# Attention and expert layer: all shared tiles first, routed results added to the output in place

## The reference

```python
x = x + xattn(layernorm(x), ctx, ...)
h = layernorm(x)
shared = gelu(h @ shared_up) @ shared_down                # 256 -> 1024 -> 256
probs = softmax(h @ router_w)                             # 8 experts
top_k_prob, top_k_idx = top_k(probs, 2)
routed = sum over the two chosen e of gate[e] * (gelu(h @ routed_up[e]) @ routed_down[e])
out = x + (shared + routed + h)
```

## Time and profile before

| | |
|---|---|
| time, median of 3 executions | 2223.13 us (2220.79 to 2226.14) |
| time of the profiled execution | 2221.47 us |
| its span in the profile | 2219.8 us |
| mean granted clock of TensorE | 0.995 |
| TensorE busy (matmuls) | 2157.2 us, 97% |
| VectorE busy | 1799.5 us, 81% |
| ScalarE busy | 1351.4 us, 61% |
| GpSimd busy | 293.9 us, 13% |

### The profile page before, as it was taken

One profiled execution on the slowest core, in us unless ns is written; L12 is line 12 of the kernel. 1 busy time (PEld: TensorE's weight loads), 2 busy tenths in 40 slices (PEclk: granted clock), 3 DMA queues, 4 the chain that ended last, 5 costly groups with the idle time before them and its releaser, 6 DMA issues. The chain is left out here.

```text
span 2219.8 us, 48796 instructions
## 1 busy us (share of the span) xinstructions
PE 2157.2 (97%) x18002; PEld 1579.6 (71%) x18002; DVE 1799.5 (81%) x2416; ACT 1351.4 (61%) x1914; POOL 293.9 (13%) x300
## 2 busy tenths in 40 slices
PE   6999999999999999999999999999997999999998
PEld 5666666666666666666666666655886999999997
DVE  7999989899899988989989998897534555557777
ACT  6675676567567566656756755564443555567773
POOL 2110000011011000000100100001572121121120
PEclk9999999999999999999999999999998999999999
DMA  7235335334423523533442363132563434336656
GB/s 265 89 116 163 89 111 176 91 95 145 133 86 121 175 80 98 177 102 97 129 145 88 102 197 91 49 110 87 200 227 117 133 129 136 133 126 221 225 186 267
DMA packets 149314, 305.62 MB, mean 138 GB/s; under 512 B 34784, under 2 KB 71776, under 8 KB 146080
## 3 DMA queue, kind: packets, MB, share of 16 engines
q1 hardware_dynamic: 138688, 272.46, 39.2%
q0 software_dynamic: 10176, 30.45, 3.8%
q10 hardware_dynamic: 288, 0.26, 0.0%
HBM read 189.31 MB, written 79.20 MB: 121 GB/s over the span
## 5 line engine op out<-in xcount | busy, mean ns | idle before, releaser
L1030 ACT ACTIVATE probs<-scores 128x1024 f32<-128x1024 f32 x512 | 503.3, 1025 | 331.6 <-PE scores L745 326.3
L871 PE MATMUL sum_ps<-probs,v_nat 128*64 128x512 f32 x2056 | 479.2, 599 | 9.3 <-DVE probs L1229 9.3
L1335 DVE TENSOR_TENSOR sums<-sums,probs 128x1024 f32<-128x1024 f32 x384 | 470.2, 1224 | 12.5
L745 PE MATMUL scores<-q_split,k_split 64*128 64x512 f32 x3072 | 415.5, 395 | 1.8 <-ACT probs L1030 1.8
L1229 DVE TENSOR_SCALAR probs<-probs 128x2048 f32<-128x2048 f32 x256 | 313.1, 1223 | 100.5 <-ACT probs L1030 99.1
L1917 PE MATMUL sum_ps<-down,hid_split 128*128 128x256 f32 x2640 | 353.8, 284 | 7.5 <-DVE acc L2060 3.9
L1917 PEld LDWEIGHTS sum_ps<-down,hid_split 128*128 128x128 f32 x2640 | 341.1, 191 | 26.2 <-issue 7.3
L1894 PE MATMUL scores<-xT,up 128*128 128x512 f32 (+1 forms) x1680 | 348.1, 349 | 0.0
L745 PEld LDWEIGHTS scores<-q_split,k_split 64*128 64x128 f32 x3072 | 282.6, 185 | 57.0 <-ACT probs L1030 5.9
L2051 DVE TENSOR_TENSOR hid_split<-hid,hid_split 128x512 fp32r<-128x512 f32 x205 | 142.1, 693 | 217.9 <-ACT hid_split L1981 217.4
L871 PEld LDWEIGHTS sum_ps<-probs,v_nat 128*64 128x64 f32 x2056 | 134.2, 136 | 240.0 <-issue 188.4
(11 more groups left out here) (228 smaller groups left out, 2186.8 us busy)
## 6 DMA issues: line engine op xcount, KB each, us to landing
k_two<-k_two SPq DMA_DIRECT2D x252, 128.0 KB, 2.3
w_all<-wpack SPq DMA_DIRECT2D x60, 512.0 KB, 4.3
raw<-L_ffn_routed_up SPq DMA_DIRECT2D x27, 1024.0 KB, 5.4
raw<-L_ffn_routed_down SPq DMA_DIRECT2D x27, 1024.0 KB, 5.2
rden<-rden_rows SPq DMA_DIRECT2D x128, 128.0 KB, 2.9
ctx_parts<-stage SPq DMA_DIRECT2D x28, 512.0 KB, 3.4
ctx_all<-ctx_parts SPq DMA_DIRECT2D x14, 1024.0 KB, 7.2
sorted_rows<-zero POOLq DMA_DIRECT2D x64, 162.5 KB, 2.5
```

The costliest lines, as they stand in the source:

```text
L745: last = pe.matmul(scores[j % 2][:, head], k_split[i][own, a, j * P:(j + 1) * P], q_split[i][own, m], start=n == 0, stop=n == 2)
L871: last = pe.matmul(sum_ps[64 * head:64 * head + 64, p % 2], v_nat[p // 2 % 2][:, j, cols:cols + 64], probs[:, j % PROBS, head], start=j == ...
L1030: act.activation(probs[:, j % PROBS], scores[j % 2][:], ACT.Exp, scale=float(HD) ** -0.5).then_inc(s_exp, 1)
L1335: v.tensor_tensor(to, to, probs[:, j % PROBS], ALU.add).then_inc(s_add, 1)
```

## The change

All eight shared tiles come first, and `late` is gone. Each batch is stored to the output as soon as its shared result is added; the sums of batches 6 and 7 use the buffers of batches 0 and 1 again, once these are stored. The sorted rows carry two more values, the second gate and the difference of the two gates, from which `address` makes each row's weight. A routed result is multiplied by its weight as it leaves PSUM: for a small tile by two ScalarE instructions of 128x256, for a big tile by these two and one VectorE instruction for the other half (`weighed`, with its own semaphore `s_yv`). GpSimd then adds the rows to the output itself by indirect transfers with an addition, after all eight stores. `returned_rows`, the gathers, `combine` and the second load of the shared weights are gone. The output tensor has 512 more rows for the padding of the tiles; they are cut off outside.

```diff
-    LATE = 2
-    HEAD = B - LATE
+    HEAD = B
...
+    acc = [t[:] for t in (acc0, acc1, acc2, acc3, acc4, acc5)]
+    ACCS = len(acc)
+    out_rows = out[0:B * N].rearrange("(b p t) d -> b p t d", b=B, p=P)
...
+        last = [small(SMALL // 2 - 1, 0), small(SMALL // 2 - 1, 1), small(SMALL // 2, 0), None, None]
+        for n in range(3):
             body(*last[n:n + 3])
...
+            sp.dma_start(out_rows[b], acc[b % ACCS]).then_inc(s_out, 16)
...
+            if b > 0:
+                store(b - 1)
+            if b == 2:
+                sp.wait_ge(s_out, 16 * (b + 0))
+                for n in range(ACCS, B):
+                    load_acc(n)
+        store(HEAD - 3)
         sp.wait_ge(s_scatall, 1)
         for i in range(2):
             load_rows(row_of(i, False), i, False)
+        for b in range(HEAD - 2, HEAD):
+            store(b)
...
-        sp.wait_ge(s_wlo, FT * ROUTED - FT // 2)
-        load_up(ROUTED % 2, shared_up[0])
-        sp.wait_ge(s_wlo, FT * ROUTED)
-        load_down(ROUTED % 2, shared_down[0])
-        for n in range(LATE):
-            sp.wait_ge(s_up, small(SMALL // 2, 0).c0 if n == 0 else late(0).c0)
-            load_part(HEAD + n, (ROUTED + n) % 2)
-        sp.wait_ge(s_tr, ROUTED)
-        sp.wait_ge(s_dest, ROUTED)
-        for b in range(HEAD, B):
-            load_acc(b)
         sp.wait_ge(s_back, 64 * BIG + 32 * SMALL)
-        sp.wait_ge(s_wlo, FT * ROUTED + FT)
-        def store(b):
-            sp.dma_start(out[b].rearrange("(p t) d -> p t d", p=P), acc[b]).then_inc(s_out, 16)
-        for b in range(B):
-            src = ys[2 * (b * N + 1):2 * (b * N + N + 1)]
-            sp.dma_start(gat[b], src.rearrange("(p t n) d -> p t n d", p=P, n=2)).then_inc(s_gat[b], 16)
-        for b in range(B):
-            sp.wait_ge(s_part_added, 2 * QT * (b + 1))
-            if b == B - 1:
-                sp.wait_ge(s_comb, 1)
-            store(b)
         sp.wait_ge(s_out, 16 * B)
...
+        pool.wait_ge(s_out, 16 * B)
         def give_back(t):
             pool.wait_ge(s_dest, t.r + 1)
             pool.wait_ge(s_y, t.T + 1)
+            if not t.half:
+                pool.wait_ge(s_yv, t.r + 2)
             for q in range(QT // 2 if t.half else QT):
-                pool.indirect_dma_start(ys, bass.IndirectOffsetOnAxis(ap=dest[t.u][:, q:q + 1], axis=0),
-                                        y_sb[t.u][:, q], None).then_inc(s_back, 16)
+                pool.indirect_dma_start(out, bass.IndirectOffsetOnAxis(ap=dest[t.u][:, q:q + 1], axis=0),
+                                        y_sb[t.u][:, q], None, compute_op=ALU.add).then_inc(s_back, 16)
             pool.wait_ge(s_back, 64 * (t.r + 1) if not t.half else 64 * BIG + 32 * (t.r + 1 - BIG))
             pool.sem_inc(s_free, 1)
...
+                if t.r is not None and (not t.half or isinstance(t.r, int) and t.r == BIG):
+                    pe.wait_ge(s_yv, t.r + 1)
...
                 act.wait_ge(s_free, t.r + 1)
-                q = QT // 2 if t.half else QT
-                act.activation(y_sb[t.u][:, 0:q], yp[:, 0:q], ACT.Copy).then_inc(s_y, 1)
+                act.wait_ge(s_dest, t.r + 1)
+                for q in range(QT // 2):
+                    last = act.activation(y_sb[t.u][:, q], yp[:, q], ACT.Copy, scale=weight[t.u][:, q:q + 1])
+                last.then_inc(s_y, 1)
...
+        v.tensor_copy(meta[:, :, 2], gate[1][:])
+        v.tensor_tensor(meta[:, :, 3], gate[0][:], gate[1][:], ALU.subtract)
...
-            mine, second = rows[n.u][:, 0:q, D], rows[n.u][:, 0:q, D + 1]
+            mine, first, second, more = (rows[n.u][:, 0:q, D + c] for c in range(4))
             v.scalar_tensor_tensor(aside[:, 0:q], mine, 0.0, spare[:, 0:q], ALU.is_equal, ALU.mult)
-            v.scalar_tensor_tensor(whither[:, 0:q], second, tile_e[:, bass.ds(n.r, 1)], mine, ALU.not_equal, ALU.add).then_inc(s_addr, 1)
+            v.scalar_tensor_tensor(chosen[:, 0:q], first, tile_e[:, bass.ds(n.r, 1)], more, ALU.is_equal, ALU.mult).then_inc(s_addr, 1)
             v.wait_ge(s_addr, n.r + 1)
-            v.tensor_tensor(dest[n.u][:, 0:q], whither[:, 0:q], aside[:, 0:q], ALU.add).then_inc(s_dest, 1)
-        added = [0]
-        def combine(count):
-            for _ in range(count):
-                b, n, t = added[0] // (2 * QT), added[0] // QT % 2, added[0] % QT
-                if t == 0:
-                    if n == 0:
-                        if b >= HEAD:
-                            v.wait_ge(s_y, late(1).T)
-                        v.wait_ge(s_gat[b], 16)
-                    else:
-                        v.wait_ge(s_part_added, added[0])
-                q = b * QT + t
-                v.scalar_tensor_tensor(acc[b][:, t], gat[b][:, t, n], gate[n][:, q:q + 1], acc[b][:, t],
-                                       ALU.mult, ALU.add).then_inc(s_part_added, 1)
-                added[0] += 1
-        PARTS = 2 * QT * B
-        COMBINE = {(0, f): 5 for f in range(5, FT + 1)} | {(1, f): 5 for f in range(2, FT - 1)}
-        BETWEEN = 3 * QT
+            v.scalar_tensor_tensor(dest[n.u][:, 0:q], mine, -1.0, aside[:, 0:q], ALU.add, ALU.add)
+            v.tensor_tensor(weight[n.u][:, 0:q], chosen[:, 0:q], second, ALU.add).then_inc(s_dest, 1)
+        def weighed(t):
+            h = QT // 2
+            v.wait_ge(s_dn, t.c0 + t.steps)
+            v.wait_ge(s_dest, t.r + 1)
+            v.tensor_tensor(y_sb[t.u][:, h:], yp[:, h:], weight[t.u][:, h:].unsqueeze(2).broadcast_to((P, h, D)), ALU.mult).then_inc(s_yv, 1)
...
+                if t.batch is None and not t.half and f == t.steps + 1:
+                    weighed(t)
                 hidden(t.c0 + f, f)
...
-                if is_late(t):
-                    combine(COMBINE.get((t.batch - HEAD, f), 0))
             if t.batch is not None:
-                if n is None:
-                    combine(PARTS - added[0])
-                    v.wait_ge(s_part_added, PARTS)
                 shared_sum(t)
-                if is_late(t) and n is not None:
-                    combine(BETWEEN)
```

More of the change, by code:

```diff
@@ L1473, in expert_tables @@
     QT, NT, ROUTED = sh.QT, sh.B * sh.QT, sh.BIG + sh.SMALL
-    return (sb("spare", [P, QT]), sb("aside", [P, QT]), sb("whither", [P, QT]), [sb(f"dest{i}", [P, QT], I32) for i in range(2)],
+    return (sb("spare", [P, QT]), sb("aside", [P, QT]), sb("chosen", [P, QT]), [sb(f"weight{i}", [P, QT]) for i in range(2)], [sb(f"dest{i}", [P, QT], I32) for i in range(2)],
             sb("e_less", [P, sh.E]), sb("meta", [P, NT, sh.DW - sh.D]), [sb(f"gate{i}", [P, NT]) for i in range(2)],
@@ L1477, in expert_tables, with experts @@
             sb("tile_ei", [P, ROUTED], I32), sb("tile_at", [P, ROUTED], I32))
-def experts(nc, sh, es, mem, att, start, xn_d, xnT, xs, ys, shared_up, shared_down, routed_up, routed_down, out, ident, logits, tables):
+def experts(nc, sh, es, mem, att, start, xn_d, xnT, xs, shared_up, shared_down, routed_up, routed_down, out, ident, logits, tables):
     KD, QT, D, B, N, E, F = sh.KD, sh.QT, sh.D, sh.B, sh.N, sh.E, sh.F
@@ L1499, in sem @@
         return es.enter_context(nc.semaphore(name))
-    spare, aside, whither, dest, e_less, meta, gate, idx, tile_u, tile_e, tile_ei, tile_at = tables
+    spare, aside, chosen, weight, dest, e_less, meta, gate, idx, tile_u, tile_e, tile_ei, tile_at = tables
     done = att["done"]
@@ L1534, in experts @@
     xT = [xT0, xT1]
-    acc = [t[:] for t in (acc0, acc1, acc2, acc3, acc4, acc5)] + [t[:, :, 0:D] for t in rows]
+    acc = [t[:] for t in (acc0, acc1, acc2, acc3, acc4, acc5)]
+    ACCS = len(acc)
+    out_rows = out[0:B * N].rearrange("(b p t) d -> b p t d", b=B, p=P)
     scores, sum_ps, proj = att["psum"]
@@ L1548, in routing @@
         return ap.rearrange("p (a b) -> p a b", b=shape[1])
[L1551 to L1554, removed]
     stage = [t[:] for t in rows] + [t[:, h * QT * DW:(h + 1) * QT * DW].rearrange("p (t d) -> p t d", d=DW)
@@ L1607, in experts @@
     s_back, s_free = sem("f_back"), sem("f_free")
-    s_gat = [sem(f"f_gat{b}") for b in range(B)]
-    s_part_added = sem("f_part_added")
-    s_comb = sem("f_comb")
+    s_yv = sem("f_yv")
     s_out = sem("f_out")
@@ L1622, in small @@
                     r=k * 2 + (BIG + i), k=k + BIG // 2)
[L1624 to L1631, removed]
     def weights_of(t):
@@ L1649, in tiles @@
             body(small(k, 1), small(k + 1, 0), small(k + 1, 1))
-        last = [small(SMALL // 2 - 1, 0), small(SMALL // 2 - 1, 1), small(SMALL // 2, 0), late(0), late(1), None, None]
-        for n in range(5):
+        last = [small(SMALL // 2 - 1, 0), small(SMALL // 2 - 1, 1), small(SMALL // 2, 0), None, None]
+        for n in range(3):
             body(*last[n:n + 3])
     def own_weights(t):
-        return t is not None and t.r is not None and t.batch != HEAD + 1
-    assert BIG % 2 == 0 and SMALL % 2 == 1 and LATE == 2 and HEAD % 2 == 0
+        return t is not None and t.r is not None
```

(22 more changed lines are left out.)

1 line of the change is left out of this document (removed).

## The result

The changed kernel takes 2216.07 us (median of 18 runs, 2211.52 to 2222.72), the kernel before 2224.48 on the same chip (18 runs). The ratio is 0.9969, interval 0.9961 to 0.9977: faster, by 6.9 us by this ratio (the two medians alone differ by 8.4) and not by the 17.1 forecast. The time of 2206.0 was wrong and so was the range, whose upper end was 2214.5. The profiled execution after took 2221.24 us with a span of 2219.6, which happens to be almost the span before. So the two profiles must be compared stage by stage: the unchanged attention stage ends 10 us later in this one than in that of before (first shared sum at 1582.64 and 1572.63).

A forecast was written before the change was run, and what follows sets the result against it. TensorE's own products plus the places where it stands still were taken as the bound. Terms -12.6 - 2.7 - 1.0 - 1.8 + 0 + 1.0 = -17.1 us took the median 2223.13 to 2206.0, range 2202.5 to 2214.5.

The forecast's parts named there:

- The tail: From last product to end of kernel: 6.1 us before, 7.1 forecast; +1.0 us, between -0.3 and +4.8.
- 0.3 to the end: Last piece of the kernel's end: 0.3 us from the landing of GpSimd's last scatter to the end.
- the stall with its slow clock: TensorE's wait for the first routed tile's sorted rows, and slow running after it, both go: -12.6 and -2.7 us.
- SyncE's reordered queue: Stores of tiles 6 and 7 stand ahead of the first weight refill, which goes out about 1740: priced at nothing.
- late tiles: Two shared tiles at the end, 47.3 us, move to the front, where they take 46.4: -1.0 us.
- the 10.3 at which they would: Small tiles: accumulating scatters may take up to 10.3 us to land before delaying address operations; term 0.
- routed tiles: Evictions from PSUM: big tiles -1.8 us (between +0.6 and -1.9), small tiles 0, up to +2.0.
- small boundaries: Eviction of small tiles by two ScalarE instructions, just hidden at 0.88 us: term 0, up to +2.0 over 14 boundaries.
- big boundary: Eviction split between VectorE and ScalarE removes 0.15 us lost at each of 12 boundaries; up products 2.82 us apart: -1.8.
- C: Slower: accumulating scatters not pipelined, 19 us each, delaying address operations in 13 small tiles: +116, or 2322 us; chance 0.06.
- B: Stall moved: store 7 and refills crowd at 1740, third expert's up weights arrive 5 us late; 2213 us, chance 0.07.
- A: Nothing won at routed boundaries: weighed copies near 1.08 us, small tiles lose 0.14 each, tail +3; 2212.4 us, chance 0.12.

The follow-up runs named there:

- the first job: Changed kernel unedited (0.9971), not waiting for its last scatters (0.9952) or with plain scatters (0.9977); kernel before with GpSimd waiting for the last store (1.0034).

## Why the prediction was wrong

**The tail is the failed step**, and in it the words "0.3 to the end". It took the time from GpSimd's last landing to the end from what lay behind the last store in the kernel before, and there GpSimd had long finished. The DRAIN of GpSimd was in that trace, 9.2 us long from 2175.0, and no row of it was read, since it cost nothing there. The change makes GpSimd the last to finish. Piece by piece, forecast and measured: last product to first issue 1.74 and 1.64; to the second issue 1.26 and 1.86, since an accumulating scatter takes GpSimd 1.55 us and not 0.96; landing 3.8 and 3.7; to the end 0.3 and 6.2. Sum 7.1 and 13.4, so the term is +7.4 and not +1.0. With this one term right the forecast would have been 2212.4, within its own range.

**Right, by the profiled pair:** the stall with its slow clock -15.65 (forecast -15.3); SyncE's reordered queue 0 (no wait for raw weights or rows appears); late tiles -1.0 (47.3 us at the end before, two tiles of 23.18 in front now). GpSimd's scatters, read-add-write or not, never hold anything in the routed stretch: landing 3.6 to 8.8 us, under the 10.3 at which they would. Of the landing alone, the estimate from the Trainium skill (DMA: Bandwidth & Descriptors, Rules for kernel authors, and Latency and other measured facts) was 3.3 to 4.5 us at the end, and the trace agrees with 3.7.

**Mis-sized:** routed tiles, -1.8 forecast, -0.95 measured (from the last sum of the head to the last small product: 457.71 us after, 458.66 before, there to the 2166.4 that the prediction worked out). The small boundaries lose nothing, as taken. At a big boundary the up products still stand 2.92 us apart, from the timeline after, and not 2.82:

```profile
1795.45 1.55 PE L1871 MATMUL scores<-xT,up 128*128 128x512 f32 x6
1796.84 1.70 PE L1897 MATMUL sum_ps<-down,hid_split 128*128 128x256 f32 x12
1798.37 1.55 PE L1871 MATMUL scores<-xT,up 128*128 128x512 f32 x6
```

ScalarE is done 0.2 us before the down products at 1796.84 start, so it is probably not the copy that they wait for; what it is was not tried.

**The sum:** -15.65 - 0.95 - 1.0 + 7.4 = -10.2 for the expert stage. Two timings of the whole kernel say -6.9 and -6.5 by their ratios, -8.4 and -5.9 by their medians. Two to four microseconds are thus not explained by any step of the prediction. They stand in the profiles as a later end of the attention stage; that the place of buffers causes it was tested on other chips and not confirmed by the timings. The cause of this part stays open.

**The rivals:** none came true. C, the accumulate that is not pipelined, is excluded by the landings. B's 2213 is nearest, but TensorE has no second stall. A's 2212.4 had the tail at +3, but for a late landing, and it lost time at the small boundaries, where nothing is lost. The rival that should have been there was the plainest: the end moves to another engine, and that engine has its own closing.

**The state of the other chips** was not in the prediction either: it took the stall of one profile for a property of the kernel. Where TensorE is held back while the scatters run, the terms are 0 - 0.95 - 1.0 + 7.4 = +5.5. The unedited kernel measured +8.0 to +9.8, the four runs with a buffer put back +5.2 to +7.7.

## What to carry to other kernels

Before moving the work that ends a kernel, list for each engine when its own closing instruction starts and how long it takes, in the kernel before: the engine that will end last brings it to the end. If that is GpSimd, leave something for the others to do behind its last DMA: in these kernels some 10 to 12 us, the landing (3.7 or 2.4), 0.6 and the DRAIN (5.4 or 9.2); one shared tile of 23 us covered it. A stall won in one profile is a gain only where the lateness that causes it is the same: here TensorE's own progress up to the end of the scatters decides, and it differed between the chips by 57 to 68 us.

## What the runs showed of the hardware

GpSimd's closing DRAIN took 5447 ns in each of the 15 profiles where it had waited for all its accumulating scatters, and 9.1 to 9.2 us in the other five: behind plain scatters, or where it had not waited for the last accumulating ones. Why is open. GpSimd's issue of a 128-row indirect scatter took 1555 ns with an addition and 960 without; the landing took 5.4 or 5.5 us in the median against 3.7 or 3.8, and the kernel without the addition was not faster. On three of the four chips of the five jobs, TensorE stood still for most of the time during 64 indirect scatters in a row, mostly without a wait that the profile shows ("issue"), at a granted clock of 0.54 to 0.71 in the mean from 1610 to 1690 us. Against the chip of the first job, where the same code ran at full rate, the kernel before took 43 to 53 us more and the changed kernel 58 to 66 more; the difference is the stall of 15 us that only the first chip has.
